# The passage from attention to the feed-forward layers rebuilt, and reciprocals moved to the end of their slots

## What is computed

```python
x = x + layernorm(attn(layernorm(x), w_q, w_kv, w_out, b_out, scale))   # x: 8 x 512 x 256, 16 heads of 64
x = x + layernorm(ffn(layernorm(x)))
# attn: q, k = l2norm(q) * exp(scale), l2norm(k); softmax(q k^T) v, heads joined, @ w_out + b_out
# ffn:  h = silu(tlin(x, w1) * s1) * (tlin(x, w2) * s2)     256 -> 1024, twice
#       h = gelu(tlin(h, h1) * t1); h = gelu(tlin(h, h2) * t2)     1024 -> 1024
#       tlin(h, w3) * s3                                     1024 -> 256
```

## Time and profile before

| | us |
|---|---|
| median of 3 runs (lowest, highest) | 1771.5 (1770.7, 1775.7) |
| the profiled execution | 1771.3 |
| its span in the trace | 1769.4 |
| TensorE matmuls busy | 1703.3 (96%) |
| VectorE, ScalarE, GpSimd busy | 1184.2, 1010.7, 461.4 |

### The profile page before, as it was taken

One profiled execution on the slowest core, in us unless ns is written; L12 is line 12 of the kernel. 1 busy time (PEld: TensorE's weight loads), 2 busy tenths in 40 slices (PEclk: granted clock), 3 DMA queues, 4 the chain that ended last, 5 costly groups with the idle time before them and its releaser, 6 DMA issues.

```text
span 1769.4 us, 24647 instructions
## 1 busy us (share of the span) xinstructions
PE 1703.3 (96%) x8584; PEld 1421.9 (80%) x8584; DVE 1184.2 (67%) x2033; ACT 1010.7 (57%) x1349; POOL 461.4 (26%) x557
## 2 busy tenths in 40 slices
PE   5999999999999999999999987999999999999998
PEld 4788888788888888888888775788888888888887
DVE  5777877877877877877877876635454545445454
ACT  4877778778778777777778765223223231323231
POOL 3533533533533533533633321000000000000000
PEclk9999999999999999999999999999999999999999
DMA  4545555456455456455455653300000000000000
GB/s 130 131 116 127 123 126 139 108 126 143 103 132 138 104 130 150 105 126 123 101 117 131 149 153 100 116 2 4 22 24 1 24 1 25 0 25 1 24 1 24
DMA packets 73473, 151.44 MB, mean 86 GB/s; under 512 B 27904, under 2 KB 28288, under 8 KB 73344
## 3 DMA queue, kind: packets, MB, share of 16 engines
q1 hardware_dynamic: 65712, 122.87, 29.2%
q10 hardware_dynamic: 6624, 23.21, 4.5%
q0 software_dynamic: 1008, 3.67, 0.5%
HBM read 56.91 MB, written 20.19 MB: 44 GB/s over the span
## 4 chain that ended last, share of the span: by engine, by line
PE 76%; DVE 8%; DMA 6%; issue 5%; ACT 3%; SPq 2%; POOL 1%; DVEq 0%; ACTq 0%; POOLq 0%
PE bank L1061 15%; PE pair L1139 13%; PE pair L1140 13%; PE bank L1003 10%; PE pair L1044 4%; PE pair L1045 4%; PE bank L1075 4%; PE pair L1130 3%; PE pair L1131 3%; DVE Pl L714 3%; PE bank L1030 2%; DMA Dp<-work 2%; PE bank L1168 2%; PE bank L1169 2%; DMA work<-rows 1%
## 5 line engine op out<-in xcount | busy, mean ns | idle before, releaser
L1139 PE MATMUL pair<-hh,f 128*128 128x512 f32 x1024 | 400.7, 391 | 2.6 <-DVE hl L832 2.2
L1140 PE MATMUL pair<-hl,f 128*128 128x512 f32 x1024 | 399.5, 390 | 0.0
L1061 PE MATMUL bank<-Ph,V 128*128 128x512 f32 x1024 | 367.3, 399 | 20.9 <-DVE Pl L714 19.1
L501 ACT ACTIVATE P<-pair,sh 128x1024 f32<-128x1024 f32 x256 | 286.3, 1118 | 159.8 <-PE pair L1045 136.3
L714 DVE TENSOR_TENSOR Pl<-P,Ph 128x1024 fp32r<-128x1024 f32 x256 | 315.4, 1232 | 0.3
L1003 PE MATMUL bank<-w,xh 128*128 128x256 f32 (+1 forms) x1024 | 285.3, 341 | 6.1 <-DVE turned L708 2.8
L549 ACT ACTIVATE hr<-pair,ct 128x512 f32<-128x512 f32 x128 | 88.3, 690 | 355.0 <-PE pair L1140 355.0
L506 ACT ACTIVATE Ph<-P 128x1024 fp32r<-128x1024 f32 x256 | 271.9, 1062 | 8.1
L1061 PEld LDWEIGHTS bank<-Ph,V 128*128 128x128 f32 x1024 | 192.9, 188 | 83.8 <-issue 38.9
L1139 PEld LDWEIGHTS pair<-hh,f 128*128 128x128 f32 x1024 | 192.8, 188 | 46.6 <-DVE hl L832 5.9
L1140 PEld LDWEIGHTS pair<-hl,f 128*128 128x128 f32 x1024 | 192.8, 188 | 39.9
(11 more groups left out here) (104 smaller groups left out, 2660.3 us busy)
## 6 DMA issues: line engine op xcount, KB each, us to landing
stack<-turned SPq DMA_DIRECT2D x128, 384.0 KB, 4.0
stack<-turned SPq DMA_DIRECT2D x128, 256.0 KB, 4.7
work<-rows SPq DMA_DIRECT2D x128, 128.0 KB, 2.9
f<-raw ACTq DMA_DIRECT2D x22, 512.0 KB, 4.9
raw<-in_h ACTq DMA_DIRECT2D x16, 512.0 KB, 4.0
xt<-in_x SPq DMA_DIRECT2D x8, 512.0 KB, 8.2
xr<-in_x SPq DMA_DIRECT2D x8, 512.0 KB, 4.6
x<-xr SPq DMA_DIRECT2D x8, 512.0 KB, 5.7
```

The costliest lines, as they stand in the source:

```text
L501: e.activation(M.P[:, i % 2, :], M.SB[i % 2][:, :], ACT.Exp, bias=M.sh[:, h:h + 1]).then_inc(S["exp"])
L1061: d = e.matmul(M.OB[:, :], v, p[:, u % 3, j * 512:(j + 1) * 512], start=jt == 0 and m == 0, stop=jt == 3 and m == 2)
L1139: e.matmul(ps, w, M.hh[src][:, k, :].bitcast(to), start=k == 0, stop=False)
L1140: d = e.matmul(ps, w, M.hl[src][:, k, :].bitcast(to), start=False, stop=k == KH - 1)
```

## The change

- `invert` comes after V's low part and the scaling of q and k in its slot, no longer right after `p_low`; the reciprocal of the last pair is in the first layer.
- SyncE: the stack copies of the odd head of an odd pair come one slot later (i % 8 == 2), behind `take_sums`; x of batch 2 and later is loaded in slot 27 two batches ahead, x of batch 1 in slot 3; the load of xv of batch 0 goes to ScalarE's queue, a slot later.
- GpSimd does `normal`, `o_high` and `o_low` of the last three pairs (`LATE`), and `norm3b` of batch 0.
- Three counts leave the last slots for the first layer; other counts are spread over earlier slots; weight pieces 12 to 21 are loaded in the layers' groups.
- The slot loops of VectorE and TensorE end at slot 257. The first layer of batch 0 has one branch over all its groups, with `high0` and `halves` a tile behind `gate` as in the other batches; Silu's table is loaded in slot 256.
- Output part 31 comes after the second layer's group 1, its addition to y at VectorE's group 4 there, and the end of attention for batch 7 (`finish`, `finish2`) at group 6 and at the third layer's group 3.
- `last_tiles(0)` goes under the branch of the other batches.

```diff
@@ -18,9 +18,9 @@
...
-HEAD = NU + 2
...
 FLAG_AT = (246, 257)
...
+LATE = NP - 3
...
@@ -194,17 +190,14 @@
-LOADS = (223, 226, 227, 231, 234, 235, 239, 242, 243, 247, 250, 251) + tuple(NU + 3 + n for n in range(10))
-COUNTS = (228, 230, 231, 238, 243, 244, 246, 247, 248, 252, 253, 254)
+LOADS = (223, 226, 227, 231, 234, 235, 239, 242, 243, 247, 250, 251)
+COUNTS = (228, 230, 231, 235, 238, 239, 244, 246, 247)
...
     return n if r == 0 and 0 <= n < PIECES else None
...
-MS = ((0, 1), (2,), (3,), (4,), (5,), (6,), (7,))
@@ -316,23 +309,24 @@
...
             stack(pair_of(i), 0)
-        if i and pair_of(i - 1) is not None:
-            stack(pair_of(i - 1), 1)
+        late = 2 if i % 8 == 2 else 1
+        if i >= late and i % 8 in (2, 6) and pair_of(i - late) is not None:
+            stack(pair_of(i - late), 1)
...
             store_rec(i // 4 - 1)
-        if i - NU == 10:
-            store_x1(B - 1)
...
             store_x1(pb)
-        if b + 1 < B and i32_ == 0:
-            load_x(b + 1)
+        if i == 3:
+            load_x(1)
+        if b + 2 < B and i32_ == 27:
+            load_x(b + 2)
...
             load_xr(b)
-        if i == NU - 11:
-            load_xv(0)
-    free4(q)
+    load_xv(1)
+    free3(q)
     e.dma_start(M.s3b[:, :], M.s3).then_inc(S["s3"], 16)
-    for b in range(1, B):
+    store_x1(B - 1)
+    for b in range(2, B):
@@ -374,8 +368,30 @@
...
         q.wait_ge("on", 2 * n + 2)
-        q.wait_ge("out", 2 * (n // 2) - 2)
+        q.wait_ge("out", 2 * (n // 2))
         e.tensor_copy(M.nh[:, n % 2, :], M.on[:, n % 2, :]).then_inc(S["nh"])
...
+    def normal(n):
+        q.wait_ge("nl", n - 1)
+        for odd in range(2):
+            own = slice(64 * odd, 64 * odd + 64)
+            q.wait_ge(f"rb{n % 2}{odd}", 16 * (n // 2 + 1))
+            q.wait_ge("ev", 2 * n + odd + 1)
+            q.wait_ge("on", 2 * n + odd)
+            e.tensor_tensor(M.on[own, n % 2, :], M.Ev[own, (2 * n + odd) % 4, :], M.Rb[own, n % 2, :],
+                            ALU.mult).then_inc(S["on"])
...
+    def o_low(n):
+        q.wait_ge("nh", n + 1)
+        q.wait_ge("out", 2 * (n // 2))
+        e.tensor_tensor(M.nl[:, n % 2, :], M.on[:, n % 2, :], M.nh[:, n % 2, :].bitcast(f32),
+                        ALU.subtract).then_inc(S["nl"])
...
+    def norm3b(t):
+        q.wait_ge("rd3", 1)
+        free1(q)
+        e.tensor_scalar(M.xn[:, t, :], M.xv[:, 0, t, :], M.mv[:, t, 0:1], M.rd[:, t:t + 1],
+                        ALU.subtract, ALU.mult).then_inc(S["xn3"])
@@ -416,7 +432,11 @@
...
         if i % 4 == 1 and 0 <= i // 4 - 2 < NP:
+            if i // 4 - 2 >= LATE:
+                normal(i // 4 - 2)
             o_high(i // 4 - 2)
+            if i // 4 - 2 >= LATE:
+                o_low(i // 4 - 2)
@@ -427,10 +447,11 @@
...
             out_root(pb)
-        if i - NU == 8:
-            out_root(B - 1)
-        if i == NU - 7:
+        if i == NU - 6:
             norm_root3(0)
+            for t in range(NT):
+                norm3b(t)
+    out_root(B - 1)
@@ -525,6 +546,11 @@
...
         e.dma_start(M.place[n].bitcast(f32), M.raw[n]).then_inc(S[f"f{n}"], 16)
...
+    def load_xv0():
+        q.wait_ge("x1", 16)
+        free0(q)
+        e.dma_start(M.xv[:, 0, :, :], M.x1[0]).then_inc(S["x10"], 16)
@@ -590,10 +616,11 @@
...
             turn_high(pair_of(i), 0)
-        if HEAD <= i < HEAD + 7:
-            for m in MS[i - HEAD]:
-                gate(0, 0, m)
-                high0(0, m)
+        if i == NU:
+            q.wait_ge("cst", 64)
+            e.activation(M.pre[:, :], M.sc["s1"][:, 0:1], ACT.Silu).then_inc(S["pre"])
+        if i == NU - 10:
+            load_xv0()
@@ -602,8 +629,6 @@
...
         for n in range(3):
-            if n == 0 and b == 0:
-                continue
@@ -612,9 +637,13 @@
...
                     high0(b, m - 1)
+                if b == 0 and n == 0:
+                    load_piece(FIRST[2] + m)
+                if b == 0 and n == 1 and m in (4, 5):
+                    load_piece(FIRST[3] + m - 4)
...
             x3_high(b + 1)
-            q.wait_ge("pre", b)
+            q.wait_ge("pre", b + 1)
...
@@ -876,9 +905,9 @@
...
     head_scale(NT)
-    for i in range(SLOTS):
+    for i in range(NU + 2):
         g, c, b, r, live = slot(i)
-        i32_, pb, tail, n = i % 32, i // 32 - 1, i - NU, i // 4 + 1
+        i32_, pb, n = i % 32, i // 32 - 1, i // 4 + 1
@@ -888,11 +917,9 @@
...
             split_wo(i - 5 if i < 7 else i - 10)
-        if i % 4 == 2 and 0 <= n - 3 < NP:
+        if i % 4 == 2 and 0 <= n - 3 < LATE:
             o_low(n - 3)
-        if i % 4 == 3 and 0 <= n - 2 < NP:
-            invert(n - 2)
-        if early and 0 <= n - 3 < NP:
+        if early and 0 <= n - 3 < LATE:
@@ -914,37 +941,24 @@
...
             head_scale(u)
-        if i % 4 == 1 and not early and 0 <= n - 3 < NP:
+        if i % 4 == 1 and not early and 0 <= n - 3 < LATE:
             normal(n - 3)
+        if i % 4 == 3 and 0 <= n - 2 < NP:
+            invert(n - 2)
...
             add_part(quad_of(i), 1)
-        if tail == 8:
-            for t in range(NT):
-                finish(B - 1, t)
-        if tail == 9:
-            for t in range(NT):
-                finish2(B - 1, t)
-        if HEAD <= i < HEAD + 7:
-            for m in MS[i - HEAD]:
-                gate(0, m)
-                halves(0, 0, m)
...
             count_piece(COUNTS.index(i))
-        if i - 1 in FLAG_AT:
-            flag(FLAG_AT.index(i - 1))
-        if i in (NU - 9, NU - 8):
-            norm3(0, 2 * (i - NU + 9))
-            norm3(0, 2 * (i - NU + 9) + 1)
-        if i in (NU - 6, NU - 5):
-            norm3b(0, 2 * (i - NU + 6))
-            norm3b(0, 2 * (i - NU + 6) + 1)
+        if i == FLAG_AT[0] + 1:
+            flag(0)
+        if i in (NU - 8, NU - 7):
+            norm3(0, 2 * (i - NU + 8))
+            norm3(0, 2 * (i - NU + 8) + 1)
...
         for n in range(3):
-            if n == 0 and b == 0:
-                continue
@@ -954,6 +968,21 @@
...
                     halves(b, n, m - 1)
+                if b == 0 and n == 0 and m in (1, 2, 3):
+                    count_piece(8 + m)
+                if b == 0 and n == 0 and m == 4:
+                    invert(NP - 1)
+                if b == 0 and n == 0 and m == 6:
+                    flag(1)
+                if b == 0 and n == 1 and m == 4:
+                    add_part(NQ - 1, 0)
+                    add_part(NQ - 1, 1)
+                if b == 0 and n == 1 and m == 6:
+                    for t in range(NT):
+                        finish(B - 1, t)
+                if b == 0 and n == 2 and m == 3:
+                    for t in range(NT):
+                        finish2(B - 1, t)
@@ -1140,17 +1169,25 @@
...
-    def groups(b, n, ms):
+    def first_layer(n, rounded):
...
+        for m in range(KH):
+            group(0, n, m, rounded)
+            if n == 1 and m == 1:
+                outp(NQ - 1, 0)
+                outp(NQ - 1, 1)
+            if m == 5:
+                flag_sum(n + 1)
...
+    def first_batch(n):
...
         with e.If(word != 0):
-            for m in ms:
-                group(b, n, m, False)
+            first_layer(n, False)
...
         with e.Else():
-            for m in ms:
-                group(b, n, m, True)
+            first_layer(n, True)
@@ -1169,17 +1206,6 @@
...
-    def last_layer(b):
-        q.wait_ge("flag", 4)
-        word = e.value_load(M.flag[0:1, 3:4].bitcast(i32))
-        seen = dict(q.seen)
-        with e.If(word != 0):
-            last_tiles(b, False)
-        q.seen = dict(seen)
-        with e.Else():
-            last_tiles(b, True)
-        q.seen = seen
@@ -1195,10 +1221,12 @@
...
         with e.If(word != 0):
+            last_tiles(0, False)
...
         with e.Else():
+            last_tiles(0, True)
@@ -1232,16 +1260,11 @@
...
             turn3(0)
-        if HEAD <= i < HEAD + 7:
-            groups(0, 0, MS[i - HEAD])
-        if i in FLAG_AT:
-            flag_sum(FLAG_AT.index(i))
-    for n in (1, 2):
-        groups(0, n, range(6))
-        flag_sum(n + 1)
-        groups(0, n, range(6, KH))
+        if i == FLAG_AT[0]:
+            flag_sum(0)
+    for n in range(3):
+        first_batch(n)
     turn3(1)
-    last_layer(0)
```

6 lines of the change are left out of this document (2 added, 4 removed).

## The result

The changed kernel takes 1766.8 us (median of 11 runs, 1761.2 to 1770.7) where the kernel before takes 1774.2 beside it (11 runs, 1767.7 to 1777.7): a ratio of 0.9965, with a 95% interval of 0.9953 to 0.9977. By the ratio that is 6 us, about a third of the 17.4 forecast. The profiled execution of after took 1769.67, 2.9 more than its median and only 1.6 less than that of before, so of differences between the two traces of a few us the runs have the last word.

A forecast was written before the change was run, and what follows sets the result against it. TensorE was taken as the bound, with at most 27 us to win in the passage and seven times 2.5 in attention. Terms 2.5 + 3.6 + 3.8 + 0 + 7.5 = 17.4 off 1771.3 gave 1753.9, range 1743 to 1767.

The forecast's parts named there:

- Start of a batch: Attention, batches 1 to 6: denominators go out sooner, so TensorE's waits for Pl at batch starts go; 5.0 us won.
- Reciprocals last: Attention, slot 27: reciprocal 2.8 us later delays its multiplication; 0.4 us of TensorE in six batches, 2.5 lost (0 to 14).
- rival B: Slots 11, 23, 27 of seven batches: late reciprocals starve the multiplications, 25 us lost, total 1776, slower; chance 0.06.
- Slot 245: End of attention: new SyncE order removes VectorE's 4.02 wait and TensorE's 2.49; 3.6 us won with clock.
- Slots 248 to 250: Passage: new SyncE order removes VectorE's 3.48 wait and TensorE's 2.62 for the flag's copy; 3.8 us won with clock.
- Slots 250 to 257: Last slots: GpSimd's slower chain for the last three pairs against VectorE relieved of counts; net 0, -7 to +3.
- Rival A: Output parts: GpSimd's 512-wide operation takes 3.0 us and sets the pace, 10.4 us later, total 1764; chance 0.15.
- First layer: Batch 0's first layer, to the second's first matmul: shrinks from 26.9 to 16.8 us; 10.1 won.
- rival C: Larger bodies of layers two and three: each jump costs 2.01 us idle and 0.9 of clock, total 1760; chance 0.12.
- Second layer: Batch 0's second layer: third flag's sum waits until the output part's bank is read; 1.6 us added.
- The 1.6 before the last output part: Second layer: TensorE waits 1.6 us (0 to 6) for the late bounce and GpSimd's chain before output part 31.
- The jump over the seven batches: Ahead of last_tiles(0): the jump's 2.01 us of TensorE idle time stay; the small branch that goes is worth 0.1.

The follow-up runs named there:

- recip_first: The changed kernel with the reciprocals put back ahead of V and the scaling on VectorE: 1760.5 us, ratio 0.9921.
- sync_alone: The kernel before with only SyncE's moves (second stack copies later, next x loaded in slot 27), reciprocals left in place: 1755.3 us, ratio 0.9890.
- recip_sync: The kernel before with the change's whole attention part, late reciprocals plus SyncE's moves: 1767.4 us, ratio 0.9957.
- stack_alone: The kernel before with only the second stack copies moved a slot later, behind the denominators: 1759.0 us, ratio 0.9907.
- load_only: As no_branch, but with the flag's word still loaded into TensorE's register ahead of each layer: 1745.7 us, ratio 0.9833.
- outp_out: Changed kernel, early reciprocals and flag, GpSimd two pairs, flag-sum bank and last reciprocal moved; small branch bodies, last output part outside them: 1747.1 us, 0.9848.
- no_branch: Changed kernel, early reciprocals and flag, GpSimd two pairs, flag-sum bank and last reciprocal moved; batch 0's layers without flag-word load or branch: 1745.5 us, 0.9844.

## Why the prediction was wrong

The direction was right; the time was 13 us too low. The sum started from 1771.3, and the kernel before takes 1774.2 beside after; measured against that, 17.4 were forecast and 6 to 7 came. By its own steps:

- **Start of a batch: 5.0 won. Too small, and right in kind.** The waits went, and SyncE's moves alone give 1.86 us in each of six batches, 11.2. I had counted only the waits of over half a microsecond that have a row of their own; the earlier trace rows had 2.5 us of idle time in a batch, and two thirds of that went.
- **Reciprocals last: 2.5 lost. This step failed.** It is the term of rival B, and the mechanism of B was right: VectorE stands 2.5 us where I had 2.3 as the most, and TensorE 1.3 at slot 31 of batch 0. Slots 13, 25 and 29, where B looked for it, are as long as before. Its price is 6 to 8 us in the pair after and recip_first, 12 in sync_alone and recip_sync; the bounds of the term held, but the 2.5 did not. I had taken the places with slack as free, though the multiplication at 285.10 in the earlier trace rows only told that the bounce had come in by then, not by how much. B as a whole did not come true, for 12 is short of the 20 from which it decides. Batch 0, where I put nothing, is in this sum.
- **Slot 245: 3.6. Right**, to a tenth: the stretch went from 6.74 to 3.11, and stack_alone shows the cause I gave. But 1.5 of it came back two slots on, where TensorE waits 1.53 for Pl at 1041.58; in sync_alone it waits 1.49 in the same slot, and in before not at all. **Slots 248 to 250: 3.8. Wrong.** The stretch from 246 to 250 is 1.5 shorter. TensorE's 2.62 for the flag fell to 0.43, and slots 248 and 249 are 3.8 shorter, but slot 247 is 3.0 longer, with the new 1.53 and 1.27 ahead of the scores behind it. VectorE lost its wait only in part (it still stood 2.77 at 1047.67).
- **Slots 250 to 257: 0, from -7 to +3.** It was 5.1 lost, within the bounds, and for other reasons than I gave: 2.1 of it is the branch before the first layer, and the wait before output part 30 came 3.52 long where Pl had been 2.78 late. GpSimd's 64x512 multiplication takes 1.27 us, and 1.86 to 2.04 for the pair that lies beside VectorE's work; I had 1.8. The bounce took 8.9 instead of 6.5. Rival A, a slow GpSimd, is wrong: the longest such row is 2.3 us.
- **First layer: 10.1 won. This is the other step that failed.** The 6.03 us did go, and the groups themselves were near the forecast: 18.5 us from 1087.39 to the end of the last group at 1105.9, where I had 16.8. What took the gain are the branches: 4.77 before the second layer, and 2.12 before the first, with slow clock behind each (0.78 from 1087.3 to 1095, 0.50 from 1110 to 1115). That is rival C, to which I gave 0.12, and for which I priced each jump at 2.9; it had them ahead of layers two and three, and they came ahead of one and two. I had argued against it that no such wait stands at the smaller branches of before. That was true, and no evidence: the change's body before the second layer is larger, and the last output part, which it stands on, came inside.
- **Second layer: 1.6 for the third flag's sum. Right:** 1.79 at 1139.98, and it went when the bank was changed. The 1.6 before the last output part did not come, since TensorE was later still.
- **The jump over the seven batches: stays at 2.01. Wrong on the good side:** 0.64 and 0.70 are left of it.

The Trainium skill (Runtime: NRT & Kernel Launch, Instruction fetch mechanics) says that a taken branch whose target is beyond the two pages at hand waits for a fetch. The runs agree with its first half: the waits go with the branch and not with the load of the word (load_only). Its size rule was what I had left open. By our runs 192 instructions of TensorE in the body cost nothing ahead of the second layer and 240 cost 2.57 or more; but 128 cost 2.1 to 2.9 ahead of the first layer, and 256 ahead of the third cost nothing in after. No run here tells what the difference between these places is.

## What to carry to other kernels

Before putting a batch of work under one branch, see which engine runs dry there: the jump cost TensorE 2 to 5 us each, and the same work in smaller bodies, with what needs no branch left outside (both at once, in outp_out), cost none before the layers. When two edits attack the same wait, time each alone. Here the order of DMAs on the queue was the remedy, and the move of the reciprocal, which looked harmless because its own wait went, started a chain 2 to 3 us later, which its user could not always hide, least of all where a load of x stood in that chain. A wait's row tells what it costs where it stands; the slot-to-slot time tells what it costs altogether.

## What the runs showed of the hardware

- The store of the reciprocals (4 KB), which the read-back waits for, took very different times: from issue to issue 1.4 to 3.6 us before 940 us in after (2.1 at 300.53), and 4.0 to 5.0 in six of the ten from then on, when weight pieces are loaded too (5.0 at 1061.28, 4.0 at 1102.64). That this traffic is the cause is likely, but no run tested it.
- TensorE's gap at a branch has no releaser in the trace, or names whatever ended last. It was 2.1 to 2.9 us before the first layer in the five kernels with one large body there, and 2.6 to 5.0 before the second in the eight whose body there has 240 or 304 instructions; outp_out, no_branch and load_only have neither.
- GpSimd's tensor_tensor over 64x512 takes 1.25 to 1.31 us alone, and 1.86 to 2.31 where it overlaps VectorE's subtraction for Pl by 0.9 us or more. The Trainium skill (SBUF — State Buffer, Who interferes with whom) says that a VectorE instruction with two SBUF inputs and a GpSimd instruction that reads SBUF exclude each other. The traces agree: in after GpSimd's two multiplications at 1069.92 and 1071.95, shown above, and the two rows of VectorE below end at 1070.64, 1071.78, 1072.87 and 1073.99, in turn and 1.1 us apart, and the second Pl took 1.66 us where most take 1.2. Beside a count, which reads one input, GpSimd's row stayed at 1.29 (flag_early).

```profile
1069.42 1.22 DVE L743 TENSOR_TENSOR Pl<-P,Ph 128x1024 fp32r<-128x1024 f32 x1
1071.21 1.66 DVE L743 TENSOR_TENSOR Pl<-P,Ph 128x1024 fp32r<-128x1024 f32 x1 [0.57 <-ACT Ph L527]
```
